# TensorE's signals in two gather passes: from the last product to a drain behind it

## The chip, the cores and the metric

One NeuronCore of a Trainium2 chip runs the whole program. The number that counts is the device time of one execution in microseconds (us). Of the kernel before, three executions took 2756.91, 2765.78 and 2768.17 us, a median of 2765.78 us. One further execution was recorded by the hardware profiler, and all rows below come from it.

## What is computed

Two layers of a graph network over 6250 nodes and 100,000 edges that are sorted by their target node `dst`. Both are followed by a residual and a layer norm.

```python
# layer 0
msgs = z[dst] @ Wd + z[src] @ Ws + edge_weight[:, None] * ww[None, :] + bm
agg = segment_max(msgs, dst)                 # 0 where a node has no edge
x = layernorm(x + relu(x @ W1a + agg @ W1b + b1) @ W2 + b2)
# layer 1
h = x @ node_fc_W + node_fc_b
he = edge_attr @ edge_fc_W + edge_fc_b
a = sum(h[src] * h[dst], axis=-1)            # one score for each edge
t = relu(einsum('ed,mdf->emf', he, rel_att_W1) + rel_att_b1)
g = sigmoid(einsum('emf,mf->em', t, rel_att_W2) + rel_att_b2)
alpha, beta = segment_softmax(a, dst), segment_softmax(g, dst)
# weighted sums of h[src] over the edges of a node, by alpha and by each beta,
# two small products, relu, a sigmoid gate, residual, layernorm
```

## The kernel before

The program has five phases: tables, **runs** (`phase_runs`, the first gather pass), a phase over nodes, **edges** (`phase_edges`, the second gather pass), and a last phase over nodes. Each gather pass fetches 784 tiles of 128 rows of 128 floats from HBM with indirect DMAs that GpSimd (POOL) issues. Four tiles are a group, so each pass has 196 groups.

**First pass.** `runs.gather` (L209) is issued by POOL four times a group. VectorE (DVE) adds the weighted row `ww` (L850) and takes a running maximum (L861). Beside it, for each unit of two groups, TensorE (PE) and ScalarE (ACT) work out the edge gates: `mlp(u)` multiplies the edge features three times (m = 0, 1, 2; L642) into one of two pairs of PSUM banks and signals `tm` after each m; ACT's `relus` (L747) waits for `tm`, writes the result and signals `ra`; `dots(u)` (L654) waits for all three relus and signals `dt`; ACT copies the result out (L769) once `dt` has come. PE's order is `mlp(u + 1)`, `dots(u)`, and then, in the first half, a product that counts edges of a node block (`owner_rows`, L663 and L664, signal `sel`). Near the end other products come in (L672 to L704). POOL reads the same signals: from unit 12 on it waits, ahead of some gathers, until `tm` of the unit before has reached a count, and `dt` of four units back.

**Second pass.** The loop body is written out for eight groups and repeats. For each step q the engines work on different groups. PE's order is:

- `turn_rows(q + 4)`: transposes the four gathered tiles (L1338), signal `tp`, for ACT's copy (L1411) and POOL
- `scores(q + 3)`: products of node columns with the rows (L1346), signal `sT`, for DVE's `lowest` (L1513) and for ACT
- `spread(q + 2)`: one small product (L1355), signal `vv`, for DVE's `references` (L1546 to L1552)
- `turn_weights(q + 1)`: a transpose (L1361), signal `pt`, for ACT's copy (L1452) and POOL
- `sums(q)`: eight products (L1369 and L1372, each a pair of instructions for each of four, so 16 rows in the trace), signal `ug`, for DVE's `add_windows` (L1570, four each group), ACT and POOL

POOL's `gather_rows` (L462) waits for `tp` of an earlier group, for `ug` of the group whose buffers it writes, and for `pt`. Every float32 product stands as two MATMUL instructions in the trace. Each of the signals is a semaphore increment that is attached to the last product of its step (`last.then_inc(...)`).

Of the kernel before, what the change touches and what calls it, by code (L numbers as in the profile page):

```python
# [29 lines left out]
P = 128  # L30
N, E, D, DE, M = 6250, 100000, 128, 64, 3
NT = -(-E // P)
TC = -(-NT // P)
W = 32
JC = 8
JP = JC * P
GJ = 4
# [466 lines left out]
def widths(c):  # L504

    z = min(4, NBLK - 4 * c)
    return z, z * P


def phase_runs(nc, new_sems, t, i, d, runs):  # L510

    with ExitStack() as ctx:
# [13 lines left out]
        ca, cb, rows, H = runs.ca, runs.cb, runs.rows, runs.H  # L526
# [28 lines left out]
        ident = t["ident"]  # L555
# [58 lines left out]
        def _(pe):  # L614
            pe.wait_ge(wld, 8 * 16)
            nc.tensor.matmul(bank[0][:, 0:M * P], weT, w1, start=True, stop=True)
            for m in range(M):
                last = nc.tensor.matmul(bank[1][:, m:m + 1], w1[:, m * P:(m + 1) * P], be, start=True, stop=True)
# [8 lines left out]
            for m in range(M):  # L627
                last = nc.tensor.matmul(bank[3][:, (1 + m) * P:(2 + m) * P], rel[:, m * P:(m + 1) * P], o2,
                                        start=True, stop=True)
# [4 lines left out]
            def mlp(u):  # L634

                pe.wait_ge(eld[u // UC % 2], 16 * (u // UC // 2 + 1))
                for m in range(M):
                    n = M * u + m
                    if n >= 2:
                        pe.wait_ge(ra, n - 1)  # L640
                    for h in range(2):
                        last = nc.tensor.matmul(bank[4 + n % 2 * 2 + h][:, :],  # L642
                                                wf[h * DE:(h + 1) * DE, m * P:(m + 1) * P],
                                                ea[h * DE:(h + 1) * DE, u % (2 * UC), :], start=True, stop=True)
                    last.then_inc(tm, 1)

            def dots(u):

                pe.wait_ge(ra, 3 * (u + 1))
                if u:  # L650
                    pe.wait_ge(gc, u)
                for m in range(M):
                    for h in range(2):
                        last = nc.tensor.matmul(bank[3][h * W:(h + 1) * W, :], w2m[:, m * W:(m + 1) * W],  # L654
                                                rt[u % 2][m][:, h * G4:(h + 1) * G4], start=(m == 0), stop=(m == M - 1))
                last.then_inc(dt, 1)

            def owner_rows(b):

# [38 lines left out]
            def hidden_part(c):  # L698
# [5 lines left out]
                nc.tensor.matmul(bank[2][:, 0:n], w1b, G[:, 0:n], start=False, stop=True).then_inc(h1, 1)  # L704

            mlp(0)
            for g in range(PG):
                if g % 2 == 0:
# [499 lines left out]
def phase_edges(nc, new_sems, t, i, d):  # L1208

    with ExitStack() as ctx:  # L1210
# [10 lines left out]
        rows = ca(IJ * P).rearrange("p (s f) -> p s f", f=P)  # L1221
# [3 lines left out]
        win = [ca(P) for _ in range(2)]  # L1225
        relr = ca(NG * P).rearrange("p (s e) -> p s e", s=NG)
        links = ca(2 * JP + 2, BF16)
        pen, low, PT = ([ca(P) for _ in range(2)] for _ in range(3))
        oh = ca(GJ * W).rearrange("p (j w) -> p j w", j=GJ)
        wts = [ca(GJ * 4 * W).rearrange("p (j k w) -> p j k w", j=GJ, k=4) for _ in range(2)]  # L1230
# [9 lines left out]
        start = ca(16)  # L1240
        bank, banks = t["psum"], t["banks"]
        TURNED, SCORES, WEIGHTS, BOUNDS = bank[0], bank[1], bank[2], bank[3]
        ident, pick = t["ident"], t["pick"]
        acc = t["acc"]
        U = [bank[k].rearrange("p (k j w) -> p k j w", k=4, j=GJ) for k in (4, 6)]
        Z = [bank[k][:, 0:P] for k in (5, 7)]
# [19 lines left out]
        def lap(q):  # L1266
            return q // NG + 1
# [53 lines left out]
        @block.tensor  # L1321
        def _(pe):
            pe.wait_ge(pwl, 3 * 16)
            for c in range(NC4):
                z, n = widths(c)
                if c >= 2:
                    pe.wait_ge(hcc, c - 1)
                nc.tensor.matmul(bank[5 + c % 2][:, 0:n], fc, t["hT"][:, c * G4:c * G4 + n], start=True, stop=True
                                 ).then_inc(hcp, 1)
            pe.wait_ge(hcc, NC4)  # L1330
            pe.wait_ge(gsd, 2 * M)

            def turn_rows(it, q):
                s = q % NG
                pe.wait_ge(gat[s], it * 64 + 64 * lap(q))
                pe.wait_ge(hc, it * NG + (q - 1 + 1 + CREDIT))
                for j in range(GJ):
                    last = nc.tensor.transpose(TURNED[:, j * P:(j + 1) * P], rows[:, s * GJ + j, :], ident[:, :])  # L1338
                last.then_inc(tp, 1)

            def scores(it, q):
                pe.wait_ge(hc, it * NG + (q + 1 + CREDIT))
                pe.wait_ge(wn, it * NG + (q + 1 + CREDIT))
                pe.wait_ge(mn, it * NG + (q - 1 + 1 + CREDIT))
                for j in range(GJ):
                    last = nc.tensor.matmul(SCORES[j * W:(j + 1) * W, 0:P], win[q % 2][:, j * W:(j + 1) * W],  # L1346
                                            hs[q % 2][:, j * P:(j + 1) * P], start=True, stop=True)
                last.then_inc(sT, 1)

            def spread(it, q):  # L1350

                pe.wait_ge(mn, it * NG + (q + 1 + CREDIT))
                pe.wait_ge(sl, it * NG + (q + 1 + CREDIT))
                pe.wait_ge(rf, it * NG + (q - 1 + 1 + CREDIT))
                nc.tensor.matmul(BOUNDS[:, 0:8], vals[q % 2][:, 8:9].to_broadcast([P, P]), sel[q % 2][:, 0:8],  # L1355
                                 start=True, stop=True).then_inc(vv, 1)

            def turn_weights(it, q):
                pe.wait_ge(ex, it * NG + (q + 1 + CREDIT))
                pe.wait_ge(wt, it * NG + (q - 1 + 1 + CREDIT))  # L1360
                nc.tensor.transpose(WEIGHTS[:, 0:P], PT[q % 2], ident[:, :]).then_inc(pt, 1)  # L1361

            def sums(it, q):
                s = q % NG
                pe.wait_ge(wt, it * NG + (q + 1 + CREDIT))
                pe.wait_ge(bw, it * NG + (q + 1 + CREDIT))
                pe.wait_ge(ad, it * (NG * GJ) + (q - 2 + 1 + CREDIT) * GJ)
                for j in range(GJ):
                    nc.tensor.matmul(U[q % 2][:, :, j, :], rows[:, s * GJ + j, :], wts[q % 2][:, j, :, :],  # L1369
                                     start=True, stop=True)  # L1370
                for k in range(1 + M):
                    last = nc.tensor.matmul(Z[q % 2], pick[:, M - k:M - k + P], wts[q % 2][:, :, k, :],  # L1372
                                            start=(k == 0), stop=(k == M))
                last.then_inc(ug, 1)

            def group(it, q, end):
                if q + 4 < end:
                    turn_rows(it, q + 4)
                if 0 <= q + 3 < end:
                    scores(it, q + 3)  # L1380
                if 0 <= q + 2 < end:
                    spread(it, q + 2)
                if 0 <= q + 1 < end:
                    turn_weights(it, q + 1)
                if q >= 0:
                    sums(it, q)

            over_groups(pe, group)
# [499 lines left out]
```

## Time and profile before

| | |
|---|---|
| runs shown | 2756.91, 2765.78, 2768.17 us |
| profiled execution | 2743.96 us, its span 2742.2 us |
| mean granted clock of TensorE | 0.808 of full speed |
| PE, POOL, DVE, ACT busy | 67%, 60%, 49%, 41% of the span |
| first gather pass | about 70 to 1220 us of the span |
| second gather pass | about 1375 to 2645 us of the span |

No engine is busy all the time, so shares alone do not tell what sets the time; it has to be read from who waits for whom in each pass. In rows of waits and of groups, "remote" is a wait that a semaphore ended whose releasing instruction had been over for long, and "issue" is idle time for which the profile shows no wait. The ends of matmuls are modelled.

### The profile page before, as it was taken

How to read it: one execution, taken by the hardware profiler on the slowest of the kernel's cores; microseconds unless marked ns; L12 is line 12 of the kernel's file. 1: busy time of each engine (PE TensorE's matmuls, PEld its weight loads, DVE VectorE, ACT ScalarE, POOL GpSimd, SP SyncE). 2: the span in 40 equal slices, each digit the busy share in tenths (PEclk: the TensorE clock that was granted, in tenths of full speed). 3: DMA queues.
4: the chain of work that ended last, by engine and by line, in shares of the span. 5: the costliest groups of instructions: out<-in, count | busy, mean ns of one | idle time of the engine just before them, and what ended most of it. 6: DMA issues, size and time to landing. Idle time of an engine off the chain costs nothing. (4 is left out here: it accounts for less than half of the span.)

```text
span 2742.2 us, 43228 instructions
## 1 busy us (share of the span) xinstructions
PE 1835.3 (67%) x9891; PEld 1131.7 (41%) x9891; DVE 1333.0 (49%) x5220; ACT 1117.0 (41%) x3305; POOL 1648.3 (60%) x1705
## 2 busy tenths in 40 slices
PE   3577776776767676554656776767667666666675
PEld 3222222221222222113445665656556565565565
DVE  3555555554434344324634544445445544554459
ACT  1233333333333333332444544444444444444448
POOL 3766666666767677646455655556565565655625
PEclk8798888888889798786867777777877777877788
DMA  8433333333333233322411211211222121211213
GB/s 226 167 116 125 106 118 108 118 106 123 108 105 121 87 122 108 114 87 73 129 43 48 52 50 50 53 47 54 52 50 50 52 50 52 52 49 52 54 42 114
DMA packets 115984, 235.04 MB, mean 86 GB/s; under 512 B 32910, under 2 KB 68231, under 8 KB 106423
## 3 DMA queue, kind: packets, MB, share of 16 engines
q0 software_dynamic: 52832, 109.39, 16.2%
q1 hardware_dynamic: 56522, 97.21, 9.6%
q10 hardware_dynamic: 6540, 27.42, 2.9%
q8 instruction: 36, 0.59, 0.1%
q14 instruction: 54, 0.43, 0.1%
HBM read 166.01 MB, written 67.89 MB: 85 GB/s over the span
## 5 line engine op out<-in xcount | busy, mean ns | idle before, releaser
L462 POOL DMA_INDIRECT d_region<-d_h,d_region x784 | 750.2, 957 | 549.7 <-issue 241.4
L209 POOL DMA_INDIRECT acc<-d_src_product,b_region x784 | 785.0, 1001 | 381.5 <-issue 204.6
L642 PE MATMUL banks<-acc,b_region 64*128 64x512 f32 x1176 | 340.5, 685 | 274.0 <-ACT gate_col L747 130.1
L850 DVE SCALAR_TENSOR_TENSOR acc<-b_region,acc 128x128 f32<-128x128 f32 x784 | 271.2, 346 | 364.8 <-DMA acc<-d_src_product,b_region 343.7
L1570 DVE TENSOR_TENSOR acc<-acc,banks 128x160 f32 x784 | 252.6, 322 | 346.1 <-remote 148.0
L1369 PE MATMUL banks<-d_region 128*128 128x128 f32 x1568 | 303.7, 353 | 11.6 <-issue 11.6
L642 PEld LDWEIGHTS banks<-acc,b_region 64*128 64x128 f32 x1176 | 104.9, 202 | 469.3 <-issue 180.2
L1372 PE MATMUL banks<-d_region,pick 128*128 128x128 f32 x1568 | 288.9, 341 | 11.8 <-issue 11.7
L1372 PEld LDWEIGHTS banks<-d_region,pick 128*128 128x128 f32 x1568 | 271.4, 257 | 14.7 <-issue 14.7
L1369 PEld LDWEIGHTS banks<-d_region 128*128 128x128 f32 x1568 | 268.9, 257 | 18.3 <-issue 12.8
L861 DVE SCALAR_TENSOR_TENSOR acc<-acc,b_region 128x128 f32<-128x128 f32 x784 | 270.1, 345 | 9.5 <-remote 5.7
L1355 PE MATMUL banks<-d_region 128*128 128x8 f32 x392 | 89.5, 301 | 223.9 <-DVE d_region L1552 158.3
L747 ACT ACTIVATE gate_col<-banks,b_region 128x1024 f32<-128x1024 f32 x147 | 159.3, 1112 | 163.4 <-PE banks L642 86.1
L769 ACT ACTIVATE acc<-banks 64x512 f32<-64x512 f32 x98 | 57.9, 591 | 407.8 <-remote 266.3
L747 ACT ACTIVATE acc<-banks,b_region 128x1024 f32<-128x1024 f32 x147 | 158.9, 1112 | 119.8 <-PE banks L642 64.8
L1458 ACT ACTIVATE d_region<-d_region 128x128 f32<-128x128 f32 x196 | 78.8, 402 | 283.5 <-DVE d_region L1552 177.1
L1355 PEld LDWEIGHTS banks<-d_region 128*128 128x128 f32 x392 | 75.3, 240 | 278.8 <-issue 263.7
L1338 PE MATMUL banks<-shift_ident,d_region 128*128 128x128 f32 x784 | 148.1, 321 | 36.4 <-ACT d_region L1411 24.5
L1346 PE MATMUL banks<-d_region 128*32 128x128 f32 x1568 | 95.6, 320 | 108.5 <-DVE d_region L1513 82.1
L654 PE MATMUL banks<-acc,b_region 128*32 128x512 f32 x588 | 163.7, 700 | 0.0
L1411 ACT ACTIVATE d_region<-banks 128x512 f32<-128x512 f32 x196 | 114.8, 586 | 119.8 <-remote 103.4
L654 PE MATMUL banks<-gate_col,b_region 128*32 128x512 f32 x588 | 156.8, 674 | 0.8 <-ACT acc L769 0.8
(261 smaller groups left out, 2439.0 us busy)
## 6 DMA issues: line engine op xcount, KB each, us to landing
d_runs<-acc SPq DMA_DIRECT2D x48, 1024.0 KB
acc<-ea ACTq DMA_DIRECT2D x25, 1024.0 KB
acc<-d_src_product,b_region POOLq DMA_INDIRECT x784
d_region<-d_h,d_region POOLq DMA_INDIRECT x784
d_region<-d_rel SPq DMA_DIRECT2D x49, 256.0 KB
hT<-xT SPq DMA_DIRECT2D x7, 448.0 KB, 7.0
d_src_product<-acc SPq DMA_DIRECT2D x7, 448.0 KB, 3.1
d_gates<-acc ACTq DMA_DIRECT2D x196, 6.0 KB
```

Of the source, the lines that this page charges most:

```text
L209: pool.indirect_dma_start(self.rows[:, s, j, :], None, d["B"], bass.IndirectOffsetOnAxis(self.idx[:, k:k + 1], 0)).then_inc(self.gathered[ ...
L462: pool.indirect_dma_start(rows[:, s, :], None, table, bass.IndirectOffsetOnAxis(idx[:, s:s + 1], 0)).then_inc(gathered[q], 16)
L642: last = nc.tensor.matmul(bank[4 + n % 2 * 2 + h][:, :], wf[h * DE:(h + 1) * DE, m * P:(m + 1) * P], ea[h * DE:(h + 1) * DE, u % (2 * UC), ...
L654: last = nc.tensor.matmul(bank[3][h * W:(h + 1) * W, :], w2m[:, m * W:(m + 1) * W], rt[u % 2][m][:, h * G4:(h + 1) * G4], start=(m == 0), ...
L747: nc.scalar.activation(rt[u % 2][m].rearrange("p (h e) -> p h e", h=2), two(4 + n % 2 * 2, 0, G4), ACT.Relu, bias=bf[:, m:m + 1]).then_inc ...
L850: nc.vector.scalar_tensor_tensor(rows[:, s, j, :], wwb, wgt[:, k:k + 1], rows[:, s, j, :], ALU.mult, ALU.add).then_inc(ch, 1)
L861: nc.vector.scalar_tensor_tensor(H[:, k % n, :], H[:, (k - 1) % n, :], rst[:, k:k + 1], rows[:, s, j, :], ALU.add, ALU.max).then_inc(ch, 1)
L1338: last = nc.tensor.transpose(TURNED[:, j * P:(j + 1) * P], rows[:, s * GJ + j, :], ident[:, :])
L1355: nc.tensor.matmul(BOUNDS[:, 0:8], vals[q % 2][:, 8:9].to_broadcast([P, P]), sel[q % 2][:, 0:8], start=True, stop=True).then_inc(vv, 1)
L1369: nc.tensor.matmul(U[q % 2][:, :, j, :], rows[:, s * GJ + j, :], wts[q % 2][:, j, :, :], start=True, stop=True)
L1372: last = nc.tensor.matmul(Z[q % 2], pick[:, M - k:M - k + P], wts[q % 2][:, :, k, :], start=(k == 0), stop=(k == M))
L1570: nc.vector.tensor_tensor(w, w, UZ[q % 2][:, :, j, :], ALU.add).then_inc(ad, 1)
```

## The change

At seven places the increment is taken off the last product and put on a drain instruction of TensorE that follows it: `tm` and `dt` in the first pass, `tp`, `sT`, `vv`, `pt` and `ug` in the second. Nothing else changes: the products, their order, all waits and all counts are the same. The drain is issued by TensorE's queue in its turn, and the instructions behind it come after it. That is 3 x 98 + 98 = 392 drains in the first pass and 5 x 196 = 980 in the second, 1372 in all. The signals `sel` (L664), and those of L680, L672, L696 and L704, stay on their products.

```diff
@@ mlp
                                                 ea[h * DE:(h + 1) * DE, u % (2 * UC), :], start=True, stop=True)
-                    last.then_inc(tm, 1)
+                    pe.drain().then_inc(tm, 1)
@@ dots
-                last.then_inc(dt, 1)
+                pe.drain().then_inc(dt, 1)
@@ turn_rows
                 for j in range(GJ):
-                    last = nc.tensor.transpose(TURNED[:, j * P:(j + 1) * P], rows[:, s * GJ + j, :], ident[:, :])
-                last.then_inc(tp, 1)
+                    nc.tensor.transpose(TURNED[:, j * P:(j + 1) * P], rows[:, s * GJ + j, :], ident[:, :])
+                pe.drain().then_inc(tp, 1)
@@ scores
-                last.then_inc(sT, 1)
+                pe.drain().then_inc(sT, 1)
@@ spread
                 nc.tensor.matmul(BOUNDS[:, 0:8], vals[q % 2][:, 8:9].to_broadcast([P, P]), sel[q % 2][:, 0:8],
-                                 start=True, stop=True).then_inc(vv, 1)
+                                 start=True, stop=True)
+                pe.drain().then_inc(vv, 1)
@@ turn_weights
-                nc.tensor.transpose(WEIGHTS[:, 0:P], PT[q % 2], ident[:, :]).then_inc(pt, 1)
+                nc.tensor.transpose(WEIGHTS[:, 0:P], PT[q % 2], ident[:, :])
+                pe.drain().then_inc(pt, 1)
@@ sums
-                last.then_inc(ug, 1)
+                pe.drain().then_inc(ug, 1)
```

## Rows read from the trace of the kernel before

**Rows 1.** Each engine's busy time in three stretches; PE's clock is the third last column

```profile
core 0: us, PE busy (x) PEld busy (x) DVE busy (x) ACT busy (x) POOL busy (x), PEclk, DMA share, GB/s
150.00:1200.00 1050.00, 729.56 (x2599) 226.81 (x2598) 487.79 (x1697) 357.78 (x383) 707.24 (x709) 0.87 0.35 113
1400.00:2600.00 1200.00, 830.59 (x5772) 714.38 (x5772) 591.12 (x2649) 563.52 (x2418) 708.75 (x741) 0.77 0.20 51
2619.00:2645.00 26.00, 18.58 (x138) 16.70 (x138) 17.03 (x73) 12.88 (x55) 0.00 (x0) 0.88 0.10 19
```

**Rows 2.** Groups, 150 to 1200 us: count, busy us, mean ns, idle before, releasers

```profile
L209 POOL DMA_INDIRECT acc<-d_src_product,b_region x709 | 707.2, 998 | 342.0 <-issue 183.3 <-remote 93.1 <-PE banks L642 54.0
...
L769 ACT ACTIVATE acc<-banks 64x512 f32<-64x512 f32 x89 | 52.6, 591 | 382.8 <-remote 254.0 <-PE banks L654 67.1 <-issue 61.7
```

**Rows 3.** The same, 1400 to 2600 us

```profile
L462 POOL DMA_INDIRECT d_region<-d_h,d_region x741 | 709.5, 958 | 503.8 <-issue 195.5 <-remote 157.0 <-PE banks L1372 57.5
...
L1372 PE MATMUL banks<-d_region,pick 128*128 128x128 f32 x1488 | 275.7, 343 | 11.8 <-issue 11.7
```

**Rows 4.** Waits, 1400 to 2600 us: us in total, times, longest us

```profile
DVE acc L1570 <- remote: 145.3, 49, 5.1
...
ACT d_region L1452 <- remote: 88.6, 35, 4.1
ACT d_region L1411 <- remote: 87.8, 52, 3.5
```

**Rows 5.** First pass, timelines of PE and ACT: start us, us, instruction, idle before

```profile
600.61 1.46 PE L654 MATMUL banks<-acc,b_region 128*32 128x512 f32 x6
...
607.32 2.29 PE L642 MATMUL banks<-acc,b_region 64*128 64x512 f32 x8
...
612.71 0.59 ACT L769 ACTIVATE acc<-banks 64x512 f32<-64x512 f32 x1 [9.53 <-remote]
```

**Rows 6.** Second pass, timelines of PE, then of DVE

```profile
1705.05 0.61 PE L1372 MATMUL banks<-d_region,pick 128*128 128x128 f32 x4
...
1707.02 1.15 PE L1369 MATMUL banks<-d_region 128*128 128x128 f32 x8
1708.01 0.72 PE L1372 MATMUL banks<-d_region,pick 128*128 128x128 f32 x5
1709.10 0.60 PE L1372 MATMUL banks<-d_region,pick 128*128 128x128 f32 x3 [0.37 <-issue]
...
1709.31 1.23 DVE L1570 TENSOR_TENSOR acc<-acc,banks 128x160 f32 x3 [3.08 <-remote]
```

**Rows 7.** Last gather of the second pass, then PE behind it

```profile
2617.94 0.95 POOL L462 DMA_INDIRECT d_region<-d_h,d_region  x1 [0.30 <-issue]
...
2630.55 1.06 PE L1372 MATMUL banks<-d_region,pick 128*128 128x128 f32 x8
...
2638.59 1.06 PE L1372 MATMUL banks<-d_region,pick 128*128 128x128 f32 x8
2641.57 0.33 PE L1361 MATMUL banks<-shift_ident,d_region 128*128 128x128 f32 x1 [1.92 <-ACT d_region L1458]
...
2643.14 1.91 PE L1372 MATMUL banks<-d_region,pick 128*128 128x128 f32 x8
```

**Rows 8.** One line's durations, 1400 to 2600 us: ns min/median/max

```profile
L1372 PE MATMUL banks<-d_region,pick x1488: 271/278/436, 1401.9 to 2597.6; 128*128 128x128 f32 x186
```

**Rows 9.** TensorE's drains at the ends of two phases: ns min/median/max, start us

```profile
L215 PEldq DRAIN  x1: 6357/6357/6357, 52.9 to 52.9; - x1
L512 PEldq DRAIN  x1: 380/380/380, 1226.5 to 1226.5; - x1
```

**Rows 10.** Timelines around those two drains

```profile
52.33 1.71 PE L416 MATMUL banks<-shift_ident,acc 128*128 128x128 f32 x12
...
59.25 0.69 DVE L379 COPY rel_col<-banks 128x512 f32<-128x512 f32 x1 [2.84 <-remote]
...
1226.46 0.33 PE L727 MATMUL banks<-shift_ident,b_region 128*128 128x128 f32 x1 [0.84 <-DVE b_region L930]
```

More of the change, by code:

```diff
@@ L1345, in scores @@
                 for j in range(GJ):
-                    last = nc.tensor.matmul(SCORES[j * W:(j + 1) * W, 0:P], win[q % 2][:, j * W:(j + 1) * W],
+                    nc.tensor.matmul(SCORES[j * W:(j + 1) * W, 0:P], win[q % 2][:, j * W:(j + 1) * W],
                                             hs[q % 2][:, j * P:(j + 1) * P], start=True, stop=True)
-                last.then_inc(sT, 1)
+                pe.drain().then_inc(sT, 1)
             def spread(it, q):
@@ L1371, in sums @@
                 for k in range(1 + M):
-                    last = nc.tensor.matmul(Z[q % 2], pick[:, M - k:M - k + P], wts[q % 2][:, :, k, :],
+                    nc.tensor.matmul(Z[q % 2], pick[:, M - k:M - k + P], wts[q % 2][:, :, k, :],
                                             start=(k == 0), stop=(k == M))
-                last.then_inc(ug, 1)
+                pe.drain().then_inc(ug, 1)
             def group(it, q, end):
```

## The prediction, made before the changed kernel ran

> **What bounds the kernel now.** I read the busy time by stretches first, then the groups with their idle time, the waits, and then timelines of single stalls. By the stretches [rows 1] no engine is full in either gather pass: in the first PE is busy 729.56 of 1050 us and POOL 707.24, in the second 830.59 and 708.75 of 1200. Per gather that is 1050 / 709 = 1.48 us in the first pass and 1200 / 741 = 1.62 us in the second, 6.48 us a group. POOL alone would need less: a gather instruction takes 0.998 and 0.958 us [rows 2, 3] and stands 0.30 us behind the one before [rows 7], 1.30 and 1.26 us, so 5.0 us a group in the second pass. The rest of POOL's idle time ends on PE's signals: "remote" and L642 are 147 us in the first stretch [rows 2], "remote" and L1372 are 214 us in the second [rows 3].
>
> "Remote" is the row to understand. In the first pass the products of L654 are over by 602.07 and those of L642 by 609.61, yet ACT, which waits for L654's signal, goes on only at 612.71, after 9.53 us of idle time [rows 5]. In the second, L1372 ends at 1705.66, and DVE, which adds its result, starts at 1709.31 [rows 6]. So the products are done and **the signal is held**. It lasts as long as gathers run: behind POOL's last gather at 2617.94 the sums of one group follow those of the next at (2638.59 - 2630.55) / 2 = 4.0 us [rows 7]. The same work with prompt signals takes 4.0 us a group, not 6.5.
>
> What is held? In the stall of the second pass PE itself goes on for 28 products behind the held one (4 + 8 + 2 + 1 + 8 + 5, of which rows 6 show the last thirteen), then stands still, and takes up at 1709.10, when the signals come. That looks like a queue which fills behind one entry, and the count from the product that carries the signal comes out the same, 28 to 31, in the twelve such stalls that I found in this pass. If an earlier product, one without a signal, were the stuck entry, the count would vary by up to 16. So I read it as the increment that is stuck, not the product.
>
> **What the change removes.** If the increment on a matmul is what is held, a drain with no increment before it ends on time and signals at once. First pass: POOL's floor of 1.30 us a gather against 1.48 us gives (1.48 - 1.30) x 784 = 141 us at most. But `sel` of L664 stays on its product in the first half of the pass, and L672 to L704 near its end, and a held one of these holds the next drain. I take a little over half, -80 us, with ends at -20 and -141. ACT's waits (L769 254.0 us) go too, but they are not on the path that POOL sets.
>
> Second pass: the period of 6.48 us a group falls to what is next. By POOL it can't go under 5.0 us. By PE it is 830.59 us / 186 groups (1488 / 8 rows of L1372) = 4.47 us [rows 1, 3] and the cost of five drains.
>
> **What the change adds.** 980 drains in the second pass, 392 in the first. What waits behind one is PE's own next step, and all who wait for that. Its price from below: the drain at L512 was issued with the product of L727 and took 0.380 us, the product 0.33 us [rows 9, 10], so the signal is 0.05 us later than the product's end. From above, where the next step was ready: eight products of L1372 take 1.06 us at full clock and 1.91 at half [rows 7], and one product 0.28 at the median and 0.44 at most [rows 8], so the steps are (1.06 - 0.28) / 7 = 0.11 and (1.91 - 0.44) / 7 = 0.21 us and the last product ends 0.17 or 0.23 us after its successor could have started; a first product after idle time takes 0.33 us and not 0.28 [rows 7, 10], 0.05 more; with 0.05 for the signal that is 0.27 to 0.33 us. I take 0.30 us where a step follows at once and 0.05 where PE would wait anyway. In the tail of the pass PE idles ahead of one or two of the five steps [rows 7], so a group pays 1.0 to 1.5 us. 4.47 + 1.0 to 1.5 gives 5.5 to 6.0 us; 4.0 + 1.0 to 1.5, from the tail, 5.0 to 5.5. I take 5.7, nearer to the first, since it is from 186 groups and the other from two: (6.48 - 5.7) x 196 = -153 us. The ends are 5.1 us (-270) and no gain at all. In the first pass four drains a unit cost at most 1.3 us; PE has 729.56 / 88.6 = 8.2 us of work in a unit of 11.8 us, and 9.5 is still under POOL's 10.4, so they are hidden under POOL. If POOL were not the bound they would cost 1.3 x 98 = 127 us, which is the lower end's reason.
>
> Sum: -80 - 153 = **-233 us**. Against the profiled execution (2743.96 us; its span and 1.8 us around it) that is 2511; its time is 22 us under the median of the runs, so I put the change on that: 2765.8 - 233 = **2533 us**. The ends of this case are -411 (2355) and -20 (2746).
>
> TensorE loads weights behind the running product: L1372's weights overlap its products, 714.38 us of loads beside 830.59 us of products in 1200 us [rows 1]. The Trainium skill ("TensorE: Matmul & The Clock Gate", "Step-by-step: what each phase is for") says that weight loads are pulled ahead of products in flight from a queue 64 deep. By that rule a drain costs the head start as well, one load; the stretch above has 714.38 / 5772 = 0.12 us for one, 0.6 us a group, and the sum would be 118 us less of a gain. The 0.33 us of a product after idle time, with its load ahead of it, is what I hold against it.
>
> **Rivals.** *The drain is held as well* (slower). A drain may have to wait for whatever holds the entry, product or not; then the held time, in which PE now runs on by up to 31 products, becomes PE's own. For it: the drain at L215 was issued at 52.9, when gathers ran, and took 6.36 us, to 59.26, while the products of L416 are over by 54.04 and DVE went on from their last signal at 59.25 [rows 9, 10]. So this drain did not overtake a held signal. Against it: its last product carried an increment, and the changed ones don't. Price: the longest waits on late signals in the second stretch, L1570, L1452 and L1411, are 145.3 + 88.6 + 87.8 = 322 us [rows 4], 1.7 us a group. PE then has 4.47 + 1.5 + 1.7 = 7.7 us against 6.48: +239. In the first pass ACT's L769 has 254.0 us [rows 2], 2.9 us a unit; 8.2 + 1.3 + 2.9 = 12.4 against 11.8 us: +59. Together +298, 3064 us; half of it, 2915, if POOL, held up by PE, stops sooner and so ends the holds. I put it at 3060. It decides once the five drains of a group wait over 1.2 us in sum, 0.24 us each: that is the gain of both passes, (153 + 80) / 196. The Trainium skill ("Perfetto Trace Analysis", "Per-engine timelines") has a product's increment pushed once PSUM has acknowledged its bytes; by that rule, if the acknowledgement is late, a drain has to wait for the same thing, and this rival holds. No row here shows the acknowledgement.
>
> *The clock falls* (slower). The granted clock is 0.77 in the second pass with PE busy 69% [rows 1]; every drain is a gap. At half clock a group has 20 products of L1338, L1369 and L1372 at 0.21 us, 4.2 us, the rest about 1.2 (L1346, L1355, L1361; an estimate from 31 products of which these are 20), and five drains at 0.33, 7.0 us: +102, less 80 from the first pass: 2788 us. Against it: the clock in the tail, with more waiting on others, is 0.88. It decides below about 0.6.
>
> *Little changes.* Signals are prompt, but the products that keep theirs (L664 and others) go on being stuck, or PE's waits for DVE and ACT, as that for L1458 at 2641.57 [rows 7], set the period: 2720 to 2790 us, say 2760.
>
> **Chances.** The forecast 0.50, the held drain 0.28, the clock 0.10, little 0.12. Faster by over 0.5% (about what a measurement of this kernel can tell from no change): 0.48 + 0.05 = 0.53; within 0.5%: 0.02 + 0.06 = 0.08; slower: 0.28 + 0.10 + 0.01 = 0.39. The range has to reach into the held drain: from 2400 (under it perhaps 0.05) to 3090 (above it 0.12). The forecast's own range is 2400 to 2700.
>
> **What would show it.** Right: "remote" gone from ACT L769 and DVE L1570; DVE L1570 starts some 0.05 us behind the last L1372; POOL's idle time in the second pass mostly the 0.30 us steps; a group at 5.0 to 6.0 us; drains of 0.3 to 0.6 us. The held drain: drains of several us while gathers run, and PE idle behind them, a group over 7 us. The clock: drains short, granted clock of the second pass under 0.65. I am wrong above all if the increment isn't the stuck part, since the twelve counts are all that speaks for it.

## The result, and the profile of the changed kernel

| | before | changed |
|---|---|---|
| median us (lowest to highest), 4 runs each | 2765.31 (2756.91 to 2768.17) | 3210.23 (3198.21 to 3219.49) |
| ratio, 95% interval | | 1.161 (1.156 to 1.167), slower |
| span of the profiled execution, mean granted clock | 2742.2, 0.808 | 3216.6, 0.735 |
| first pass, first product of L642 to last of L654 | 1152 | 1346 |
| second pass, first product of L1346 to last of L1372 (now L1374) | 1263, 6.44 a group | 1527, 7.79 a group |

The change costs 445 us by the medians. The spans of the two traces are 474 apart: 194 in the first pass, 264 in the second, 16 outside them. The changed kernel has a line or two more in each step, so its numbers are shifted: the drains are `tm` L645, `dt` L656, `tp` L1339, `sT` L1348, `vv` L1357, `pt` L1363 and `ug` L1376; the products of the second pass are L1338, L1346, L1355, L1362, L1371 and L1374; DVE adds at L1572, ACT copies at L1413.

Busy time by stretches, the changed kernel (answers to [rows 1]; us, then busy us and instructions of PE, PEld, DVE, ACT, POOL, then granted clock, DMA share, GB/s):

```profile
150.00:1400.00 1250.00, 805.21 (x2634) 252.55 (x2634) 488.81 (x1705) 371.16 (x388) 714.93 (x714) 0.82 0.30 96
1600.00:3000.00 1400.00, 1017.59 (x5522) 808.83 (x5521) 564.46 (x2535) 555.75 (x2315) 697.94 (x708) 0.66 0.17 42
```

POOL does the same work in more time in both: 714 gathers in 1250 us, 708 in 1400. Its groups, first pass and second (answer to [rows 2, 3]; busy us, mean ns, then idle us ahead and who ended it):

```profile
L209 POOL DMA_INDIRECT acc<-d_src_product,b_region x714 | 715.2, 1002 | 534.0 <-PEq L645 317.3 <-issue 196.0 <-PEq L656 16.7
...
L462 POOL DMA_INDIRECT d_region<-d_h,d_region x708 | 697.9, 986 | 714.7 <-PEq L1339 527.4 <-issue 172.2 <-PEq L1363 14.5
```

"Remote" is gone, as forecast, but a drain stands in its place and the wait is longer. A group's four gathers now have 714.7 / 177 = 4.04 us of idle time; before it was 503.8 / 185 = 2.72 [rows 3]. That difference, 1.3 us, is what a group grew by. Most of it is POOL's wait for the drain behind L1338 (changed kernel, 1600 to 3000 us; us in total, times, longest; answer to [rows 4]):

```profile
POOL d_region L462 <- PEq L1339: 527.4, 172, 23.9
```

Now PE and then POOL in the same stretch of the second pass, the changed kernel (start us, us, instruction, idle before):

```profile
2205.20 0.65 PE L1338 MATMUL banks<-shift_ident,d_region 128*128 128x128 f32 x4 [0.33 <-issue]
2206.08 0.42 PE L1346 MATMUL banks<-d_region 128*32 128x128 f32 x8 [0.23 <-issue]
2206.79 0.36 PE L1355 MATMUL banks<-d_region 128*128 128x8 f32 x2 [0.28 <-issue]
2207.38 0.30 PE L1362 MATMUL banks<-shift_ident,d_region 128*128 128x128 f32 x1 [0.23 <-issue]
2207.99 1.54 PE L1371 MATMUL banks<-d_region 128*128 128x128 f32 x8 [0.32 <-issue]
2209.33 1.91 PE L1374 MATMUL banks<-d_region,pick 128*128 128x128 f32 x8
2212.89 1.11 PE L1338 MATMUL banks<-shift_ident,d_region 128*128 128x128 f32 x4 [1.65 <-issue]
...
2220.86 1.11 PE L1338 MATMUL banks<-shift_ident,d_region 128*128 128x128 f32 x4 [0.35 <-issue]
```

```profile
2206.65 0.94 POOL L462 DMA_INDIRECT d_region<-d_h,d_region  x1 [2.54 <-PEq L1339]
...
2210.40 0.94 POOL L462 DMA_INDIRECT d_region<-d_h,d_region  x1 [0.30 <-issue]
2214.80 0.94 POOL L462 DMA_INDIRECT d_region<-d_h,d_region  x1 [3.46 <-PEq L1339]
```

Two things are to be seen. Behind each drain the next step starts 0.23 to 0.35 us late. And behind L1374, over by 2211.24, PE stands for 1.65 us although nothing but its own drain (L1376) is ahead of L1338: none of the eight products carries an increment, and the drain behind them is held all the same. It ends once POOL has stopped (last gather over at 2211.34), and POOL can't go on before it does: POOL waits for the signal of L1338's step, whose products now stand behind that drain. **The two engines take turns.** In the trace of before PE was five steps on, at the next group's L1369 at 1707.02, while the signal of L1372 was held from 1705.66 to 1709.31 [rows 6].

The whole stretch is like this. Of the 178 drains of L1376 from 1600 to 3000 us, 102 end over 0.3 us behind their product, every one of them with POOL standing, 0.8 to 1.5 us after its last gather ended (0.97 at the median). POOL has 184 stops, and in 94% of them the L1338 step that it waits for ends only after POOL's last gather has; in the kernel before that was 19% of 142 stops, since the products were long done and only the signal was late.

Not every product is held, though. The drains behind the small steps, L1355 and L1362, end while gathers run in 173 and 167 of 178 groups, nearly always within 0.04 us of their product. Of the four drains other than L1376, 4 in 712 end over 0.3 us late. The held ones stand behind the group's sixteen sums (L1371 and L1374): where the last of these is over while gathers run, 49 of 57 drains are held.

One turn can be added up from the rows: four gathers 4.69 us (2206.65 to 2211.34), 1.55 until L1338 starts, 1.11 for L1338, 0.80 until POOL starts, 8.15 us. Over the stretch POOL has a stop of 2.98 us (median) in practically every group, 184 in 177: 4.7 + 3.0 = 7.7. In the kernel before a stop was 2.11 us and three of four groups had one (142 in 186): 0.76 x 6.8 + 0.24 x 5.0 = 6.4. That is the change of the second pass, 6.44 to 7.79.

The first pass has fewer and longer holds: 36 of 91 drains of L656 from 150 to 1400 us end over 0.3 us late, up to 11.07 us. The turns are less strict there, as 6 of the 36 end while POOL gathers. PE of the changed kernel in one of the long ones:

```profile
603.42 2.77 PE L654 MATMUL banks<-acc,b_region 128*32 128x512 f32 x12 [0.46 <-issue]
616.23 1.65 PE L663 MATMUL banks<-b_region 128*128 128x392 f32 x2 [10.04 <-issue]
```

In [rows 5] PE had gone on to L642 in such a stall; now it stands behind L654's drain. In this part of the pass L664 still carries an increment. Behind 1265.50 us no product of the pass does, and 5 of the 13 drains of L656 are held all the same, the longest among them.

### The profile page after: what moved, and what is told of

It reads as the page before. It is cut to its first block and busy times, and to the rows that moved or that the text cites. A ratio compares the mean times of both kernels' runs of the same rounds, so it can differ in the third digit from the quotient of the medians.

```text
span 3216.6 us, 44600 instructions
## 1 busy us (share of the span) xinstructions
PE 2152.3 (67%) x9891; PEld 1293.3 (40%) x9891; DVE 1331.2 (41%) x5220; ACT 1145.2 (36%) x3305; POOL 1671.2 (52%) x1705
## 5 line engine op out<-in xcount | busy, mean ns | idle before, releaser
L462 POOL DMA_INDIRECT d_region<-d_h,d_region x784 | 771.5, 984 | 795.8 <-PEq L1339 548.6
L1572 DVE TENSOR_TENSOR acc<-acc,banks 128x160 f32 x784 | 252.5, 322 | 750.2 <-PEq L1376 666.1
L642 PE MATMUL banks<-acc,b_region 64*128 64x512 f32 x1176 | 395.7, 753 | 144.7 <-issue 129.4
L1371 PE MATMUL banks<-d_region 128*128 128x128 f32 x1568 | 369.6, 410 | 65.2 <-issue 30.4
L1413 ACT ACTIVATE d_region<-banks 128x512 f32<-128x512 f32 x196 | 117.0, 597 | 699.1 <-PEq L1339 692.3
L1371 PEld LDWEIGHTS banks<-d_region 128*128 128x128 f32 x1568 | 316.1, 299 | 113.7 <-issue 112.2
L1374 PE MATMUL banks<-d_region,pick 128*128 128x128 f32 x1568 | 337.0, 388 | 0.0
L1374 PEld LDWEIGHTS banks<-d_region,pick 128*128 128x128 f32 x1568 | 324.0, 304 | 0.0
L1338 PE MATMUL banks<-shift_ident,d_region 128*128 128x128 f32 x784 | 171.5, 357 | 215.5 <-issue 205.0
L642 PEld LDWEIGHTS banks<-acc,b_region 64*128 64x128 f32 x1176 | 105.6, 217 | 416.1 <-issue 367.3
L1338 PEld LDWEIGHTS banks<-shift_ident,d_region 128*128 128x128 f32 x784 | 111.5, 179 | 265.5 <-issue 265.5
L663 PE MATMUL banks<-b_region 128*128 128x392 f32 x98 | 59.7, 700 | 208.7 <-issue 202.2
L654 PE MATMUL banks<-acc,b_region 128*32 128x512 f32 x588 | 148.2, 640 | 36.9 <-issue 27.1
L654 PE MATMUL banks<-gate_col,b_region 128*32 128x512 f32 x588 | 147.1, 636 | 21.8 <-issue 14.3
L1346 PE MATMUL banks<-d_region 128*32 128x128 f32 x1568 | 105.9, 338 | 48.1 <-issue 48.1
L1355 PE MATMUL banks<-d_region 128*128 128x8 f32 x392 | 91.4, 306 | 59.7 <-issue 59.7
```

The costliest lines, as they stand in the source:

```text
L462: pool.indirect_dma_start(rows[:, s, :], None, table, bass.IndirectOffsetOnAxis(idx[:, s:s + 1], 0)).then_inc(gathered[q], 16)
L642: last = nc.tensor.matmul(bank[4 + n % 2 * 2 + h][:, :], wf[h * DE:(h + 1) * DE, m * P:(m + 1) * P], ea[h * DE:(h + 1) * DE, u % (2 * UC), ...
L1413: nc.scalar.activation(hs[q % 2], TURNED, ACT.Copy, scale=-1.0).then_inc(hc, 1)
L1572: nc.vector.tensor_tensor(w, w, UZ[q % 2][:, :, j, :], ALU.add).then_inc(ad, 1)
```

## The experiments

They fell on four chips, and **the kernel before is not the same on all of them**: 2737 and 2741 us where the second and third sets ran, as on the chip of the prediction (2765), but 2279, 2277 and 2281 us where the first, fourth and fifth ran, three different chips. So every run is read against the kernel before of its own set. I call the first kind a holding chip, the other an open chip. The second and third sets ran on one and the same holding chip, and each open chip was met once, so that it is the chip that decides, and not something else that changed between the sets, is likely but not shown. Ratios are with their 95% interval.

| run | chip | us | ratio | first pass | second pass (a group) |
|---|---|---|---|---|---|
| before_again | holding | 2754.7 (one) | | 1156 | 1264 (6.45) |
| after_again | holding | 3184.84 | 1.164 (1.160 to 1.168) | 1335 | 1510 (7.70) |
| e1b | holding | 2928.19 | 1.068 (1.064 to 1.073) | 1338 | 1255 (6.40) |
| x1 | holding | 2898.83 | 1.059 (1.056 to 1.063) | 1146 | 1405 (7.17) |
| x2 | holding | 2832.02 | 1.034 (1.031 to 1.038) | 1149 | 1344 (6.86) |
| e3b | holding | 3185.23 | 1.161 (1.156 to 1.167) | 1345 | 1504 (7.67) |
| e5 | holding | 1976.93 | 0.722 (0.719 to 0.725) | 748 | 897 (4.58) |
| e6 | holding | 2224.10 | 0.813 (0.807 to 0.818) | 809 | 1066 (5.44) |
| e1 | open | 2281.17 | 1.001 (0.999 to 1.002) | 953 | 992 (5.06) |
| e2 | open | 2334.67 | 1.021 (1.018 to 1.024) | | |
| e3 | open | 2388.62 | 1.044 (1.038 to 1.050) | 955 | 1091 (5.57) |
| e4 | open | 2683.17 | 1.181 (1.176 to 1.185) | 957 | 1386 (7.07) |
| e4b | open | 2700.63 | 1.186 (1.184 to 1.189) | | |
| after_third | open | 2367.20 | 1.038 (1.036 to 1.040) | 953 | 1079 (5.51) |
| x3 | open | 2280.79 | 1.002 (1.000 to 1.003) | | |
| x3b | open | 2281.22 | 1.001 (0.999 to 1.002) | | |
| x4 | open | 1939.37 | 0.852 (0.850 to 0.854) | 755 | 893 (4.56) |
| x4b | open | 1936.40 | 0.850 (0.848 to 0.851) | | |

The passes are from the traces, first product to last as in the first table; they are left out where nothing rests on them, and for e2, whose five executions lie from 2323 to 2383 us, the widest spread here, with the profiled one at 2369. Theories: **held** (a drain waits for products whose completion is held while gathers run, and PE stands with it), **serial** (each drain costs its lost overlap and a restart, wherever it runs), **clock** (the gaps bring the granted clock down).

**The first set: one pass alone, and where the signal stands.** e1 has the drains of the first pass alone, e2 those of the second alone (the same edit at `tp`, `sT`, `vv`, `pt` and `ug`):

```diff
-                    last.then_inc(tm, 1)
+                    pe.drain().then_inc(tm, 1)
...
-                last.then_inc(dt, 1)
+                pe.drain().then_inc(dt, 1)
```

> Drains in the first pass alone (tm, dt). In the changed kernel the first pass takes about 1339 us (75 to 1414 us) against 1145 before, so 2765 + 194 = 2959 us if the passes don't touch each other. Held theory (a drain waits while completions are held, and TensorE with it): drains of L656 end 2.9 us on average behind the last product's modelled end and those of L645 0.38 us, 4.0 us a unit in sum, and the pass is 190 to 200 us longer. Serial theory (a drain costs only the lost overlap and the restart, some 0.3 us each): 392 drains x 0.3 = 118 us at most, and less under POOL's cover: 2765 to 2880 us.

> Drains in the second pass alone (tp, sT, vv, pt, ug). The second pass takes about 1527 us with the change against 1270 before: 2765 + 257 = 3022 us if the passes add. Serial theory: four of the five drains end 0.02 us behind the last product, the next product starts 0.2 to 0.3 us later, TensorE's clock in the pass is at 0.66 against 0.77, and the group is at 7.8 us. Held theory: only L1376's drain (0.76 us a group behind the last product) counts, 149 of the 257 us. Both expect the time; the rows of the drains tell how much each has.

e3 leaves every signal on its product and puts a bare drain behind; e4 is the changed kernel with a second drain behind each:

```diff
                 last.then_inc(ug, 1)
+                pe.drain()
...
                 pe.drain().then_inc(ug, 1)
+                pe.drain()
```

> All signals back on the last product, and a drain without a signal behind each. If the place of the signal is what matters (the increment on a product is held, my reading before the result), signals come late as before and the drains wait for them: slower than the changed kernel, 3300 us or more. If the drains themselves are the cost, whoever signals: 3210 us within 1%. If a signal on the drain is itself dear: under 3100 us.

> The changed kernel with a second drain behind each, 1372 more. It finds the engine idle, so it has no overlap to lose and nothing held to wait for: what it adds is the price of the instruction itself. Serial theory with a restart price that is the drain's own (0.2 us): up to 1372 x 0.2 = +274 us. If the price is all in the emptying: 1372 x 0.02 to 0.05 us = +27 to +70 us, 3240 to 3280 us. Held theory: no more than +70 us.

The expectations were written against 2765 us, and this chip gives 2279. What was missing is the holding itself: in e1's second pass, which is the code of before, no wait on "remote" is left, where a holding chip has 498 us of them, these above all (before_again, 1400 to 2600 us):

```profile
DVE acc L1570 <- remote: 151.9, 43, 5.4
POOL d_region L462 <- remote: 149.8, 69, 3.0
```

and POOL stands beside its 0.30 us steps for next to nothing (e1, 1300 to 2100 us):

```profile
L462 POOL DMA_INDIRECT d_region<-d_h,d_region x630 | 608.2, 965 | 192.0 <-issue 167.9 <-PE banks L1372 14.0 <-PE banks L1338 8.2
```

So an open chip is POOL-bound at 5.06 us a group. There the drains of the first pass cost nothing (e1), those of the second 2.1% (e2). e3's 1.044 (1.038 to 1.050) is near the 1.038 of the whole change (after_third, below, on another open chip), which speaks for PE's stop as the cost and not where the signal stands; e3b, below, settles it where signals are held.

e4's second drains cost 2683 - 2367 = 316 us beside after_third (two open chips, on which the kernel before differs by 2 us). That is far more than the first ones and more than the 27 to 274 us that I had written. The second drain itself is a row of 13 ns (L1383). Most of the cost goes with **the clock**. Second pass of after_third (open chip), then of e4:

```profile
1300.00:2200.00 900.00, 679.58 (x5050) 529.39 (x5049) 514.07 (x2320) 516.26 (x2118) 632.30 (x652) 0.93 0.25 59
```

```profile
1300.00:2500.00 1200.00, 908.15 (x5230) 739.39 (x5229) 535.48 (x2404) 530.32 (x2192) 659.31 (x676) 0.72 0.19 46
```

With 31 products a group that is 163 and 169 groups: PE's busy time goes from 4.17 to 5.38 us a group, its idle time from 1.35 to 1.73. Five more drains add 0.38 us of standing still and 1.21 us of slower products, at a granted clock of 0.72 where it had been 0.93.

**The second set, on a holding chip: the change, and the drains without the gathers' density.** e5 is the kernel before and e6 the changed one, each with one gather of four behind the first lap (the other rows are stale, so this part of the input is left out; the counts that others wait for follow, and POOL's wait for `pt` now stands behind a group's one gather):

```diff
-            gathers(q, range(0, GJ // 2))
+            gathers(q, range(0, 1))
...
-                    runs.gather(pool, d, g, j)
+                    if g < RG or j == 0:
+                        runs.gather(pool, d, g, j)
```

> The changed kernel again, on whatever chip this falls to, to be read against the kernel before on the same chip. Held (the drain waits for products whose completion is held while gathers run): where the kernel before takes about 2280 us and holds nothing, the change costs what its two passes cost alone there, 0 + 55 us (e1, e2), 2320 to 2350; where it takes about 2765 us, 3210 again, 1.15 to 1.17 times. Serial (the lost overlap and the restart of 1372 drains cost it, wherever it runs): 1372 x 0.3 = 410 us on either chip, 2690 beside 2280, since PE then has as many stops in both.

> The kernel before, for its trace on the same chip. If the chip is the one where it takes about 2280 us: a group of the second pass at 5.1 us, POOL's gathers 1.30 us apart, waits of DVE L1570 and ACT L1411 and L1452 on late signals under 20 us in 1200 (322 us in the trace of the kernel before). If 2765: as that trace, 6.5 us a group.

> The kernel before, but after the first lap of the row buffers only one of the four gathers of a group is issued in either pass (the waits count 16 for 64; the second pass's gather no longer waits for PE's L1355 of a use before), the other rows are stale. So POOL needs 1.3 us a group and PE is the bound. Held: a group of the second pass as in the tail of the kernel before, 4.0 us, and a first-pass gather group near PE's 8.2 / 2 = 4.1 us: together some 1650 to 1800 us for the program. If holds come from the gathers and not from their number, 1900 or more.

> The same cut of the changed kernel, so that its difference from e5 is the price of a drain where nothing hides it and few gathers run. Serial: 980 drains in the second pass at 0.30 to 0.50 us, less those where PE waits anyway (one or two of five), 180 to 400 us, and 392 in the first at 0.3, 120 us, of which DVE and ACT hide part: 250 to 500 us over e5. Held: under 150 us over e5, since with a quarter of the gathers there is little to hold and the drains stand mostly where PE waits anyway.

The change costs 1.164 times again. With a quarter of the gathers the same chip holds nothing (no "remote" wait in e5's second pass), and PE sets the pace. So the price of a drain is bare here: second pass 1066 - 897 = 169 us for 980 drains, 0.17 us each, first pass 809 - 748 = 61 us for 392, 0.16 us each. In all 247 us by the times, at the lower edge of what I had written for *serial*, and more than *held* alone would have. My 1650 to 1800 us for e5 was too low, and 1977 falls where I had put holds that don't depend on the number of gathers (1900 or more), but the trace shows none: a group takes 4.58 us, and the 4.0 that I had from two groups of the tail doesn't hold over a pass, where PE waits for DVE's references (L1355 138.9 us in 750). POOL's instructions and the transfers are both fewer, so e5 doesn't tell which of them the holds need. The durations of one drain, from being issued to its end, tell held from not held. L656 in e6 and in the changed kernel (ns min/median/max):

```profile
L656 PEldq DRAIN  x77: 2592/2732/2742, 152.6 to 794.1; - x77
```

```profile
L656 PEldq DRAIN  x94: 2637/3330/13783, 155.5 to 1419.3; - x94
```

A drain's row begins while the products before it still run, so 2.73 us is those products and no wait; 13.78 is a hold of 11 us. On the open chip it is 2.73 at the median and 2.74 at most (e1), as with few gathers on the holding one.

**The third set, on the holding chip: which drain.** e1 and e3 again, and the second pass's drains apart: x1 has only the one behind the group's sums (`ug`), x2 only the other four.

```diff
-                last.then_inc(ug, 1)
+                pe.drain().then_inc(ug, 1)
```

> e1 again (drains in the first pass only), for a chip where signals are held (the kernel before at about 2740 to 2765 us). Held: the first pass, 1152 us before, grows as in the changed kernel, to about 1346: 1.07 times, with L656's drain ending 2 to 3 us behind its product on average. Serial: the drains' own 0.16 us (e6 less e5, first pass, 61 us in 392) stay hidden under POOL as on the other chip: 1.00 to 1.01. On the chip where nothing is held it is 1.00 again and tells nothing new.

> One drain of the five in the second pass, that behind the sums of L1372 at the group's end, nothing in the first. Held chip: if the cost is held products met by this drain, it alone costs most of the second pass's 264 us: 0.17 serial and 0.76 held a group, 150 to 200 us, 1.055 to 1.075. If it is serial only, 0.17 to 0.3 us a group, 35 to 60 us, 1.012 to 1.02. Chip with nothing held: POOL sets the pace, 1.00 to 1.01.

> The other four drains of the second pass. Held chip: held products are rarely met by these (0.04 us on average in the changed kernel), so serial only: 4 x 0.17 to 0.2 = 0.7 to 0.8 us a group, 135 to 160 us, 1.05 to 1.06, or less by what POOL's slack of the held kernel covers. If every drain makes holds longer, 200 or more, 1.07. Chip with nothing held: 1.01 to 1.02.

> e3 again (each signal stays on its last product, an unsignalled drain behind it), for a chip where signals are held. If PE's stops are the cost and where the signal stands is nothing, as the changed kernel within 2%: 1.14 to 1.18. If the drain's signal is what is late and the product's comes sooner, well below, 1.05 to 1.10. If the increments on products are held beside what the drains cost, above: 1.20. Where nothing is held, 1.04 again.

The three parts add up: 0.0684 + 0.0594 + 0.0343 = 0.162 beside 0.164 for the change. e1, which cost nothing on the open chip, costs 187 us here, as *held* has it. One drain a group (x1) costs 158 us, and four (x2) cost 91. That is under the 135 to 160 that I had written and under the bare price of theirs (784 x 0.17 = 133), so part of it goes into waits that are there anyway; I have no row that shows which. e3b equals the change: an unsignalled drain does the whole damage. The drain of x1 and the first of x2:

```profile
L1374 PEldq DRAIN  x167: 2207/5708/9930, 1495.6 to 2695.3; - x167
```

```profile
L1339 PEldq DRAIN  x173: 1843/4048/4508, 1503.1 to 2693.4; - x173
```

In x1 it ends 2.13 us behind its product on average (over 0.3 us in 155 of 166, of which 34 end while POOL gathers); on an open chip the changed kernel's L1376 ends 0.02 behind (after_third). In x2 the hold moves on to the next drain, L1339 behind L1338 (1.07 us), which in the changed kernel ends 0.02 behind. The products are the same: it is whichever drain comes first behind the group's sixteen sums that waits. A likely reason why x1 is the dear one, not shown apart, is that its drain keeps L1338 back, while that of x2 stands behind L1338, which is done by then. Of the 0.31 us between their groups POOL's idle time has 0.20, and its gathers the rest (974 and 950 ns each):

```profile
L462 POOL DMA_INDIRECT d_region<-d_h,d_region x665 | 648.0, 974 | 553.1 <-PE banks L1338 360.7 <-issue 171.7 <-remote 19.2
```

```profile
L462 POOL DMA_INDIRECT d_region<-d_h,d_region x694 | 659.1, 950 | 542.8 <-PEq L1339 348.7 <-issue 165.0 <-PEq L1363 23.2
```

that is 553.1 / 166 = 3.33 and 542.8 / 173.5 = 3.13 us of idle time a group.

**The fourth and fifth sets, meant for a holding chip; both met open ones.** x3 has the drain of L654 alone (`dt`). x4 is e5 with two of four gathers (again the other rows are stale).

> One drain of the four a unit in the first pass, that behind the sums of L654; the three of L642 keep their product's signal. Chip where signals are held: in e1 this drain ends 3.09 us behind its product on average, those of L642 0.31. If the held wait is the cost, this one alone costs most of e1's 187 us: 120 to 187, 1.045 to 1.07. If each drain adds its own part, a quarter, 47 us, 1.017. Chip where nothing is held: 1.00.

> e4 again (a second drain behind each), for a chip where signals are held. There the second drain finds nothing more to wait for. Its own price on the other chip is (2683 - 2335) us, 348, as 0.34 us in 980 drains with the first pass hidden under POOL. If that price simply adds, 3185 + 348 = 3530, 1.29 times, and somewhat more from the first pass, which is not hidden here (392 x 0.16 to 0.34 = 60 to 130): up to 3660. If the stop of the second drain takes the place of a held wait, under 3450.

> As e5, the kernel before with two of four gathers a group behind the first lap (waits count 32 for 64, the other rows are stale). POOL then needs 2.6 us a group, PE 4.6 (e5, which held nothing on this chip). If holds end when POOL stops for 1 to 2 us, as 98 of 167 releases in the trace of before_again's second pass come 0.8 to 2 us behind a gather's end, signals are held little: 1980 to 2080 us. If they grow with the number of gathers, half of the 460 us that separate the two chips come back: 2150 to 2250.

> The changed kernel, meant for the chip where nothing is held, which its own runs have not met yet. There: e1 and e2 add, 2335 to 2345 beside about 2280, 1.02 to 1.03. On a chip where signals are held, 1.155 to 1.17 as before.

> x3 again for a chip where signals are held (its first run met one where nothing is). If the wait for held products is the cost, this one drain costs most of e1's 187 us: 120 to 187, 1.045 to 1.07. If each drain of the first pass adds its own part, a quarter, 47 us, 1.017. Where nothing is held 1.00 again.

> x4 again for a chip where signals are held; where nothing is held this kernel took 1939 us, PE's own pace. If holds end when POOL stops for 1 to 2 us, within 2% of that, 1940 to 1980. If they grow with the number of gathers, half of the 460 us between the chips: 2150 to 2200.

x3, e4b and x4 could not answer here what they were made for: nothing was held. What they give is that e4 is 1.181 and 1.186 on two open chips, and that PE's own pace, 4.56 us a group in x4 and 4.58 in e5, is the same on an open and on a holding chip. after_third is the one with news: the whole change costs 3.8% on an open chip, 86 us, over the 1.02 to 1.03 that e1 and e2 had led me to write. They are all in the second pass, 1079 against e1's 992. e2's profiled execution, at 2369 us, has 1074 there, which fits; its median of 2335 lies lower, and its scatter leaves that open. PE, with 5.51 us a group, has become the bound in place of POOL's 5.06.

## Why the prediction was wrong

**The direction is wrong**, 2533 forecast and 3210 measured, and the time lies 120 us above the top of the range. Step by step:

- *What bounds the kernel* was read rightly: signals held while gathers run. It goes with the chip of the run: with nothing held, the same kernel takes 2277 to 2281 us. POOL's floor of 5.0 us a group is 5.06 there.
- *"It is the increment that is stuck, not the product."* **This is the step that failed**, and both gains, -80 and -153, hung on it. In the changed kernel's second pass no product of a group has an increment, and yet the drain behind them waits, 102 of 178 at L1376; so it is at L656 behind 1265.50 us, up to 11.07 us. What is late is the products' completion, and a drain stands until it has come; PE stands with it. The count of 28 to 31 products was no evidence. I had taken it from stalls at L1372, where the held product is also the one with the signal; a count of what gets past it can't tell which of the two is stuck. A stall that begins at a product without a signal leaves no late signal of its own and would not have been in my sample. The row that could tell was the drain at L215, 6.36 us under held products [rows 9, 10]. I had it, and set it aside because its last product carried an increment.
- *What a drain costs where PE is the bound* was 0.30 us in my sum; e6 less e5 gives 0.17. I had added up a lost overlap of 0.17 to 0.23 us, the restart and the signal. The step behind a drain does start 0.2 to 0.3 us late, but part of that is there without a drain (in the trace of before PE idled over 0.1 us ahead of L1346 in 76 of 186 groups). A group then takes 5.5 us where nothing is held, against my 5.7. That this is near is partly luck: the drains were put too high (5 x 0.17 = 0.86, not 1.2) and the group without them too low (4.58 in e5, not 4.47). It is beside the point as well: the hold, not the drain, makes the 7.8.
- *The rival of the held drain* is what happened. Its second pass, 7.7 us a group and +239 us, came out at 7.79 and +264. Its size came from waits on late signals; the turns of PE and POOL explain the number, and they were not in my text, so that the two agree is luck. Its first pass was mis-sized: 2.9 us a unit, taken from ACT's one wait, and +59; measured +194. In e1b the `dt` drain alone waits 3.09 us behind its product and the three `tm` drains 0.31 each, 4.0 us a unit. With that in its place my sum gives 13.5 us a unit, and 1346 / 98 = 13.7 was measured; but it has the four drains at 1.3 us, and at 4 x 0.16 some 0.9 us a unit is missing. The stretches have 0.6 of it: PE's busy time is 805.21 us in 91 units, 8.8 a unit where it was 8.2, at a granted clock of 0.82 and not 0.87. Some 0.3 us is unexplained. I gave this rival 0.28, and "half of it" as a softer price; the full price was still too low.
- *The clock* fell in the second pass, 0.77 to 0.66, but does not set the time there. The group from 2205.20, whose first steps run at full clock, takes 7.69 us, the next, at half clock, 7.97; over the stretch the 23 groups with L1374 at full clock take 7.8 us, those at half 7.9. With the engines taking turns, PE's speed hardly counts. Where nothing is held it is another matter, as e4 shows.
- *Little changes* fell with the first step.

The signs that I had named for the held drain are the ones that came: drains of several us while gathers run, PE idle behind them, a group over 7 us. The first is a weak one as it stands, since a drain's row begins beside its products: L656 takes 2.73 us where nothing is held. Its end less the last product's end is what tells.

Of the two pages that I had cited one bears on the failed step. The Trainium skill ("Perfetto Trace Analysis", "Per-engine timelines") has a product's increment pushed once PSUM has acknowledged its bytes, so that what a late acknowledgement delays is the product's completion; a drain that waits behind unsignalled products agrees with that, though no row shows an acknowledgement. The other page of the Trainium skill ("TensorE: Matmul & The Clock Gate", "Step-by-step: what each phase is for") has weight loads pulled ahead of products in flight. Past a drain they are not: weight loads of the changed kernel, second pass,

```profile
2209.12 1.83 PEld L1374 LDWEIGHTS banks<-d_region,pick 128*128 128x128 f32 x8
2212.89 0.72 PEld L1338 LDWEIGHTS banks<-shift_ident,d_region 128*128 128x128 f32 x4 [1.94 <-issue]
```

L1338's load begins with its product, behind the drain, where in the trace of before it began 0.11 us ahead at the median. That head start is lost, as I had weighed, but it is within the 0.17 us of e6 and not 0.12 on top of the 0.30.

**What stays open.** What holds the completion of the sums while gathers run, why the small products beside them are not held, and why it happens on one kind of chip and not on three others. It does not last until the transfers are done: when the 102 held drains of L1376 end, 11 packets of the gathers' queue are still under way at the median. Whether in the first pass the drain of L654 alone makes the loss (x3 met no holding chip), and whether half the gathers would be enough for holds (x4 likewise). And the 0.3 us a unit of the first pass.

## What to carry to other kernels

A late signal has two possible causes, a late increment or a late completion, and a drain could help at most against the first, which no run here shows; against the second it turns a delay that others see into one that TensorE stands through, with all its later products behind it. Before moving a signal, look for one drain that already stands behind such work in the trace, and take its time at face value. Count also who waits for the step behind the drain: here it was the very engine with whose stopping the holds ended in the second pass, and the two fell into step.

## What the runs showed of the hardware that I had not expected

- One kernel takes 2277 to 2281 us on three chips and 2737 to 2765 where signals are held, and a change that costs 3.8% on the first costs 16% on the second. In one set the times of the kernel before agree within 0.8%; those of e2 and e3 spread over 2.6 and 1.7%.
- A TensorE drain costs 0.16 to 0.17 us where TensorE is the bound and nothing is held (e6 less e5). In the second pass it ends 0.02 to 0.04 us behind the modelled end of its last product, and the next product starts 0.2 to 0.3 us after that.
- A second drain behind each first one is a row of 13 ns and costs 0.38 us of idle time a group and 1.21 us of slower products: the granted clock went from 0.93 to 0.72 (e4 against after_third).
- With one gather in four the holding chip holds nothing. With all of them the changed kernel's held drains of L1376 end 0.8 to 1.5 us after the last gather has; in the first pass and in x1 some end while gathers run.
- A drain behind one or two small products (L1355, L1362) ends promptly beside running gathers on the same chip, while one behind the sixteen sums is held.
